# Segment maximum by block transposes, weights and dot sums by four chunks, and VectorE's window loop written out

## The reference

```python
x = _layernorm(x + _L0_gnn_ref(x, ...))    # sum of neighbours, two 256x256 weights
x = _layernorm(x + _L1_gnn_ref(x, ...))    # two GAT layers, 4 heads
x = _layernorm(x + _L2_gnn_ref(x, ...))    # three HGT layers, 8 heads, and a dense block each
x = _layernorm(x + _L3_gnn_ref(x, ...))    # typed and weighted sum of neighbours

# GAT, once per layer
e = leaky_relu(el[src] + er[dst]); ex = exp(e - segment_max(e, dst)[dst])
out = segment_sum(z[src] * ex / segment_sum(ex, dst)[dst], dst)
# HGT, once per layer
scores = sum(Q[dst] * kt, -1) / scale * mu;  e = exp(scores - segment_max(scores, dst)[dst])
agg = segment_sum(V[src] * e / segment_sum(e, dst)[dst], dst)
```

## Time and profile before

| what | value |
|---|---|
| median of 3 executions | 7095.4 us (7089.9 to 7103.44) |
| the profiled execution, its time | 7100.4 us |
| the profiled execution, its span | 7098.4 us |
| mean granted TensorE clock | 0.787 of full |
| busy share PE, DVE, ACT, POOL | 69%, 63%, 39%, 61% |
| GAT stages in the span | about 1530 to 2230 and 2230 to 3050 us, with the dense work ahead of the second |
| HGT stages in the span | windows from 3078.6, 4201.1 and 5328.5 us on, some 730 us each |

### The profile page before, as it was taken

The page is one execution under the profiler, slowest core; times in us unless marked ns, Lnnn a source line. Parts: engine busy times, 40 slices in busy tenths (PEclk is TensorE's granted clock), DMA queues, the critical chain, the costliest instruction groups (busy, mean ns, idle before and its releaser), DMA issues. The chain is left out here.

```text
span 7098.4 us, 101999 instructions
## 1 busy us (share of the span) xinstructions
PE 4898.9 (69%) x25668; PEld 3603.3 (51%) x25669; DVE 4452.5 (63%) x10705; ACT 2794.8 (39%) x6632; POOL 4296.3 (61%) x4216
## 2 busy tenths in 40 slices
PE   3780267657775777567767977776986676896665
PEld 2670144435554555455545965554874454673343
DVE  7550222256666666879996458898448999664334
ACT  1220000036665665455554655444665455450000
POOL 0777577747774777367774247775227777216775
PEclk6665565668887888789998988889998989896665
DMA  1220133343442335255554245555225555323334
GB/s 35 97 84 5 44 99 99 99 81 104 105 99 73 105 104 98 95 175 158 163 160 93 68 129 159 159 158 128 65 90 167 160 160 159 81 90 114 98 98 90
DMA packets 353408, 771.53 MB, mean 109 GB/s; under 512 B 88772, under 2 KB 199265, under 8 KB 349745
## 3 DMA queue, kind: packets, MB, share of 16 engines
q0 software_dynamic: 213760, 613.91, 33.0%
q1 hardware_dynamic: 139441, 155.22, 6.6%
HBM read 662.95 MB, written 105.92 MB: 108 GB/s over the span
## 5 line engine op out<-in xcount | busy, mean ns | idle before, releaser
L719 POOL DMA_INDIRECT ring<-tab_kv,idx_i x1392 | 1386.6, 996 | 638.3 <-issue 386.7
L1110 PE MATMUL pp<-ring,oh 128*128 128x256 f32 x1856 | 866.3, 619 | 434.4 <-DMA ring<-tab_h,idx_i 208.4
L719 POOL DMA_INDIRECT ring<-tab_z,src_i x928 | 919.4, 991 | 380.6 <-issue 254.7
L797 PE MATMUL pp<-ring,X 128*128 128x264 f32 x2784 | 898.9, 459 | 110.6 <-DVE ring L699 96.2
L1110 PEld LDWEIGHTS pp<-ring,oh 128*128 128x128 f32 x1856 | 506.9, 300 | 793.4 <-issue 391.6
L760 PE MATMUL pq<-Qs,oht 128*128 x7020 | 749.2, 244 | 181.5 <-issue 106.1
L849 ACT ACTIVATE ohb<-iota_row,lo_s 128x128 bf16<-128x128 f32 x2360 | 751.6, 390 | 41.6 <-PEq L731 23.4
L760 PEld LDWEIGHTS pq<-Qs,oht 128*128 128x128 bf16 x7020 | 554.0, 103 | 419.7 <-issue 285.9
L797 PE MATMUL pp<-ring,scratch 128*128 128x264 f32 x1856 | 673.2, 504 | 128.8 <-DVE ring L699 127.8
L699 DVE TENSOR_TENSOR ring<-ring 128x512 f32<-128x512 f32 x899 | 698.5, 783 | 55.0 <-ACT ring L888 54.9
L1018 DVE TENSOR_TENSOR acc<-acc,pp 128x264 f32 x1160 | 491.0, 423 | 352.1 <-PE pp L797 273.7
(11 more groups left out here) (306 smaller groups left out, 8338.9 us busy)
## 6 DMA issues: line engine op xcount, KB each, us to landing
...
ring<-tab_y,src_i POOLq DMA_INDIRECT x464, 2.8
ring<-tab_h,idx_i POOLq DMA_INDIRECT x464, 2.8
```

The costliest lines, as they stand in the source:

```text
L719: nc.gpsimd.indirect_dma_start(out=ring[:, par, c, :], out_offset=None, in_=table, in_offset=bass.IndirectOffsetOnAxis(ap=idx[:, w * WC + ...
L797: last = nc.tensor.matmul(pp[p % 2][:, 0:W8], oh[:, par % 2, 2 * p + c, :], ring[:, par % RW, 2 * p + c, 0:W8], start=(c == 0), stop=(c == 1))
L1110: last = nc.tensor.matmul(bank[:, 0:D], oh[:, b, 2 * k + c, :], ring[:, b, k, c, :], start=(c == 0), stop=(c == 1))
```

## The change

- The windows' small state on one partition (`conn`, `single`, `pL`, `pR`, `rF`, `rB`, `cL`, `cR`, `inL`, `inR`) is replaced. The penalties between chunks are laid out once, ahead of the layers, as a row of 68 values per window and spread over all 128 partitions by five matmuls with ones (`link`).
- The scores are kept head first, so that partition 16h + c is head h and chunk c. VectorE's transpose of 32x32 blocks then brings the last column of the forward scan, and the first of the backward one, into the rows of partitions 0, 32, 64 and 96, two heads in each. VectorE scans these on all partitions and transposes the results back into columns. TensorE's `T2` and `T3`, ScalarE's copy of the scores (L877) and the copy of the penalties (L953) go; VectorE reads the transposed scores from PSUM. `C.wait` stands between the dependent instructions.
- The rescaling factor comes by two matmuls more: `ratio` sums the masked differences into one row, `factor` builds 1 - oh + oh*exp, in PSUM, where `rescale` reads it without the copy of L998.
- A weight instruction and a dot sum take four chunks (128x1024 elements) in place of two. In HGT POOL does one of four quads in place of three of eight pairs.
- VectorE's windows are written out 29 times; TensorE's and ScalarE's stay in the loop.
- The orders by hand are new. `C1` to `C4` are now `T1`, `ratio`, `T4`, `factor`.

```diff
+        row_l = s.sb("row_l", [1, NW, 2, LH], BF16)
+                e.wait_ge(s_l, 1)
+                for k in range(parts):
+                    n = min(LW, NW - LW * k)
+                    nc.tensor.matmul(ptr[k][:, 0:n * 2 * LH], ones_r[:, :],
+                                     row_l[:, LW * k:LW * k + n, :, :].rearrange("o w h e -> o (w h e)"), start=True, stop=True
+                                     ).then_inc(s_b, 1)
+                    L.do(nc.vector.tensor_copy(link[:, LW * k:LW * k + n, :].rearrange("p w e -> p (w e)"), ptr[k][:, 0:n * 2 * LH]))
...
+    ORDER_V_DOTS = order("S0 S1 S2 W0 t S3 A0 W1 S4 A1 S5 A2 W2 S6 A3 S7 A4 D1 A5 D2 A6 D3 A7")
+    ORDER_V_SUMS = order("W0 t W1 A0 W2 A1 A2 L A3 W3 A4 D1 A5 D2 A6 D3 A7")
+    ORDER_T_DOTS = order("Q2 Q3 G0 T2 G1 Q4 Q5 T3 G2 Q6 Q7 G3 G4 C1 G5 N0 N1 G6 G7 C2 C3 H C4")
+    ORDER_T_SUMS = order("G0 Q2 Q3 G1 T2 G2 Q4 Q5 T3 G3 Q6 Q7 G4 C1 G5 N0 N1 G6 G7 C2 C3 H C4")
...
-            on_pool = (3, 5, 7) if dots else ()
+            on_pool = (3,) if dots else ()
+            def weigh_quad(eng, par, q):
+                v = ring[:, par % RW, 4 * q:4 * q + 4, 0:D].rearrange("p c (h x) -> p c h x", h=heads)
+                return eng.tensor_tensor(v, v, bc(ring[:, par % RW, 4 * q:4 * q + 4, D:D + heads], 3, D // heads), ALU.mult)
...
-                            if w >= 2 and q < len(on_pool):
-                                weigh(w - 2, par, q)
+                            if w >= 2 and q == 1 and on_pool:
+                                weigh(w - 2, par)
...
+                    def ratio(w, par):
+                        e.wait_ge(s_G, w + 1)
+                        nc.tensor.matmul(pc[1][0:1, 0:HD], one_c[:, :], G[:, :, :].rearrange("p k h -> p (k h)"),
+                                         start=True, stop=True).then_inc(s_Gm, 1)
+                    def T4(w, par):
+                        e.wait_ge(s_exp, w + 1)
+                        nc.tensor.transpose(sc_t, S1, ident[:, :]).then_inc(s_T4, 1)
+                    def factor(w, par):
+                        e.wait_ge(s_eg, w + 1)
+                        nc.tensor.matmul(fac, one_r[:, :], one_r[:, 0:HD], start=True, stop=False)
+                        nc.tensor.matmul(fac, oh[0:1, par % 2, 0, :], neg_r[:, 0:HD], start=False, stop=False)
+                        nc.tensor.matmul(fac, oh[0:1, par % 2, 0, :], gr[:, :], start=False, stop=True).then_inc(s_fac, 1)
...
+                    def red(w, par, q):
+                        e.wait_ge(s_mul, w * NPR + (2 * q + 4))
+                        k = 2 * (q % 2)
+                        nc.vector.tensor_reduce(scw[:, par % 2, :, 4 * q:4 * q + 4].rearrange("p h c -> p c h"),
+                                                prod[:, k:k + 2, :, :].rearrange("p k c (h x) -> p (k c) h x", h=HD),
+                                                AX.X, ALU.add).then_inc(s_red, 1)
...
-                        if p:
-                            red(w, par, p - 1)
+                        if p and p % 2 == 0:
+                            red(w, par, p // 2 - 1)
...
+                    def D1(w):
+                        C.base, C.n = c_base + w * c_per, 0
+                        e.wait_ge(s_T1, w + 1)
+                        C.do(nc.vector.tensor_tensor_scan(F, pens(w, 0), sc_t, -BIG, ALU.add, ALU.max))
+                        C.do(nc.vector.tensor_tensor_scan(R[:, ::-1], pens(w, 1)[:, ::-1], sc_t[:, ::-1], -BIG, ALU.add, ALU.max))
+                    def D2(w):
+                        C.wait()
+                        C.do(nc.vector.transpose(at_c(inF, 2), two(FR[:, P - 1:P + 31])))
+                        C.do(nc.vector.transpose(at_c(inR, 2), two(FR[:, P:P + 32])))
+                        C.wait(3)
+                        C.do(nc.vector.tensor_tensor_scan(flat(outF[:, :, :]), links(w), flat(inF[:, :, :]), -BIG, ALU.add, ALU.max))
+                        C.wait(4)
+                        C.do(nc.vector.tensor_tensor_scan(flat(outR[:, :, :])[:, ::-1], links(w)[:, ::-1],
+                                                          flat(inR[:, :, :])[:, ::-1], -BIG, ALU.add, ALU.max))
+                        C.wait(5)
+                        C.do(nc.vector.transpose(two(colF[:, :]), at_c(outF, 1)))
+                        C.wait(6)
+                        C.do(nc.vector.transpose(two(colR[:, :]), at_c(outR, 3)))
+                        C.do(nc.vector.tensor_copy(inF[:, :, 0], outF[:, :, 2 * WC]))
+                        C.wait(7)
+                        C.do(nc.vector.tensor_tensor_scan(F, pens(w, 0), sc_t, colF[:, 0:1], ALU.add, ALU.max))
+                        C.do(nc.vector.tensor_tensor(dg[:, :], outF[:, :, 1], outR[:, :, 2], ALU.subtract))
+                    def D3(w):
+                        C.wait(10)
+                        C.do(nc.vector.tensor_tensor_scan(R[:, ::-1], pens(w, 1)[:, ::-1], F[:, ::-1], colR[:, 0:1], ALU.add, ALU.max))
+                        C.wait(11)
+                        nc.vector.scalar_tensor_tensor(G[:, :, :], bc(dg[:, :], 1, HD // 2), 0.0, mine[:, :, :], ALU.min, ALU.mult
+                                                       ).then_inc(s_G, 1)
+                        C.wait(12)
+                        nc.vector.tensor_tensor(S1, sc_t, R, ALU.subtract).then_inc(s_sub, 1)
...
-                    windows(first, both, last_, e, RW)
+                    first(0, 0, 1)
+                    for w in range(1, NW):
+                        both(w, w % RW, w // RW + 1)
+                    last_(NW - 1, (NW - 1) % RW)
```

More of the change, by code:

```diff
@@ L589, in _ @@
                 L.do(nc.vector.memset(pen[:, :, :], 0.0))
-                L.do(nc.vector.memset(conn[:, :], -BIG))
+                L.do(nc.vector.memset(row_l[:, :, :, :], -BIG))
+                L.do(nc.vector.memset(ones_r[:, :], 1.0))
+                L.do(nc.vector.memset(one_r[:, :], 1.0))
+                L.do(nc.vector.memset(neg_r[:, :], -1.0))
+                L.do(nc.vector.memset(one_c[:, :], 1.0))
+                L.step(nc.vector.memset(mine[:, :, :], 0.0))
+                for k in range(HD // 2):
+                    L.do(nc.vector.memset(mine[32 * k:32 * k + 1, k, :], 1.0))
+                L.do(nc.vector.memset(conn[:, :], 1.0))
                 for f, o in enumerate((src_i, idx3_i, idx8_c, w_c, lo_s, dstc)):
@@ L608, in _ @@
                 L.wait()
-                L.do(nc.vector.tensor_scalar(conn[:, 1:CH], conn[:, 1:CH], -BIG, None, ALU.mult))
-                L.do(nc.vector.tensor_scalar(single[:, :], single[:, :], -BIG, None, ALU.mult))
+                for k in range(2):
+                    at = row_l[:, :, k, 1:LH - 1].rearrange("o w (c two) -> o w c two", two=2)
+                    for n, v in ((0, conn), (1, single)):
+                        L.do(nc.vector.tensor_scalar(at[:, :, :, n], v[:, :].rearrange("o (w c) -> o w c", c=WC), -BIG, None, ALU.mult))
+                L.wait()
+                e.sem_inc(s_l, 1)
+                for k in range(parts):
+                    n = min(LW, NW - LW * k)
+                    e.wait_ge(s_b, k + 1)
+                    L.do(nc.vector.tensor_copy(link[:, LW * k:LW * k + n, :].rearrange("p w e -> p (w e)"), ptr[k][:, 0:n * 2 * LH]))
                 L.wait()
@@ L658, in attend @@
         order_t = ORDER_T_DOTS if dots else ORDER_T_SUMS
-        width = D if dots else HD
         RW = 2
@@ L693, in attend @@
             NPR = WC // 2
-            on_pool = (3, 5, 7) if dots else ()
-            on_dve = [p for p in range(NPR) if p not in on_pool]
-            def weigh_pair(eng, par, p):
-                v = ring[:, par % RW, 2 * p:2 * p + 2, 0:D].rearrange("p c (h x) -> p c h x", h=heads)
-                return eng.tensor_tensor(v, v, bc(ring[:, par % RW, 2 * p:2 * p + 2, D:D + heads], 3, D // heads), ALU.mult)
+            on_pool = (3,) if dots else ()
+            on_dve = [q for q in range(NQ) if q not in on_pool]
+            def weigh_quad(eng, par, q):
+                v = ring[:, par % RW, 4 * q:4 * q + 4, 0:D].rearrange("p c (h x) -> p c h x", h=heads)
+                return eng.tensor_tensor(v, v, bc(ring[:, par % RW, 4 * q:4 * q + 4, D:D + heads], 3, D // heads), ALU.mult)
             exs = lambda par: ring[:, par % RW, :, D:W8]
@@ L724, in _ @@
                         gathers(w, w % RW)
-                    for w in (NW - 2, NW - 1):
-                        for k in range(len(on_pool)):
-                            weigh(w, w % RW, k)
+                    if on_pool:
+                        for w in (NW - 2, NW - 1):
+                            weigh(w, w % RW)
                 @blk.tensor
@@ L1035, in first @@
                             leaky(w, par, n)
-                        chain(w)
+                        D1(w)
+                        D2(w)
+                        D3(w)
                     def both(w, par, n):
```

197 lines of the change are left out of this document (67 added, 130 removed).

## The result

The changed kernel took 7116.4 us (median of 11 runs, 7103.5 to 7123.2) beside 7099.3 us for the kernel before (11 runs): ratio 1.0023, 95% interval 1.0014 to 1.0032. It is slower, as forecast, but by 17 us where the sum said 73.

What follows compares the result with a forecast made beforehand. GAT was taken as bound by POOL's issue of gathers, HGT by a ring of VectorE and TensorE. GAT +67, HGT 0 and setup +6 made +73 us: 7168 us (slower), own range 7120 to 7215, whole range 7000 to 7240.

Steps and rivals of the forecast that it cites:

- I take 0.48 x 4 = 1.9 us, since GAT's quads stand at many phases: GAT's gathers wait for VectorE's four long weight products, 0.48 us each on average; period +1.15 us, +67 us in all.
- 0.0 us: HGT's window: VectorE's savings and the new orders' idle time cancel; 87 x 0 = 0 us, bounds -183 and +190.
- chain, with the end of the stalls in it: VectorE's HGT scan chain: -1.4 us a window by shorter work, and 0.82 us of stalls under POOL's products gone.
- turn: idle ahead of S0 to S2: HGT, between windows: S0 and S2 wait for TensorE's matmuls and register reads; +2.5 us a window, bounds +1.3 and +3.3.
- G0 late: idle ahead of A0 and S4: HGT: TensorE's G0 waits for W0, now behind S2, so A0 and S4 wait; +1.2 us a window, bounds +0.3 and +2.0.
- idle ahead of A4 to A7: HGT, VectorE: half of the idle time ahead of the `A`s lies behind the chain's hand-overs and goes; -0.5 us a window.
- the chain's gain is taken back by the turn: HGT: the chain's -1.4 us a window is offset by the new orders' +2.5 us of idle time between windows.
- The setup: The penalties' stage ahead of the layers: five copies, five matmuls, a memset and four products more; +6 us.
- POOL's stop (23.4): HGT: POOL's gathers and waits for VectorE's quads would stop a gain at a period of 23.4 us, not reached.
- Quads cost no more than pairs: Rival: GAT's gathers lose nothing to the longer products and HGT stays; 7101 us, no change; chance 0.12.
- TensorE keeps up: Rival: TensorE's sequencer runs ahead of the scores' matmuls, HGT gains 1.6 us a window; 7029 us; chance 0.28.
- Upper bounds: Rival: the turn and G0's lateness cost their upper bounds, HGT 1.2 us a window longer; 7272 us; chance 0.15.

Runs made afterwards that it cites:

- octets: The changed kernel with GAT's weights in two instructions over eight chunks each in place of four over four; 7169.0 us, ratio 1.0113.
- b_quads_2: The kernel before with GAT's weights as four instructions over four chunks, in its own order; 7167.9 us, ratio 1.0118; first run, beside 7.99 to 8.01 ms, 1.002.
- b_unrolled_2: The kernel before with only VectorE's windows written out; 7087.9 us, ratio 0.9999; first run, beside 7.99 to 8.01 ms, 0.987.
- tiles_early: The changed kernel with TensorE's windows written out and the next window's eight tile numbers read ahead of the turn; 6955.0 us, ratio 0.9812.
- pairs_w0: The changed kernel with GAT's weights by pairs of chunks again and, in HGT, W0 ahead of S2; 6832.9 us, ratio 0.9643.
- h_first: The changed kernel with the scores' twelve matmuls ahead of two transposes in HGT; ratio 1.043 beside 7.99 to 8.01 ms; repeated, 7092.3 us, 1.0009.
- w0_first: The changed kernel with W0 ahead of S2 in VectorE's HGT order; ratio 0.998, beside a kernel before of 7.99 to 8.01 ms.

## Why the prediction was wrong

Right in the main by its mechanisms, wrong by its sum: +73 forecast, +22.8 in the spans. Two terms carry the miss, -26 us in GAT and -24 in HGT.

*GAT, "I take 0.48 x 4 = 1.9 us, since GAT's quads stand at many phases": the step that failed.* The mechanism is shown: gathers take 0.994 us on average with pairs, 1.042 with quads and 1.141 with octets. By the Trainium skill's sentence (SBUF — State Buffer, Who interferes with whom), that `tensor_tensor` was not found to stall such a DMA, neither the quads nor the octets would have cost anything; the runs decide against it for these gathers. The size was off: 16 gathers came out 1.53 us a window over their undisturbed time, not 1.9, and the period grew by some 0.8 us, not 1.15; the two stages by 40.7 us, not 67. The mean over all phases holds where phases do vary: W0 to W2 of the changed kernel cost 0.47 us each on average, 0.48 predicted. W3 follows an instruction that waits for a gather to land, and stands at phases that cost little, 0.11 us. (b_quads_2 gave 1.93 for its four, as the mean would have it, but two of them stand at nearly one phase each, so that is luck.) The order in the diff (`A2 L A3 W3`) would have told it.

*HGT, "0.0 us": a sum of terms, most of them near, some short.* For the 24 windows of the second HGT stage (time occupied is from an instruction's start to the next one's, less the idle time between), us a window:

| step | predicted | measured |
|---|---|---|
| dot sums | -0.24 | -0.26 (4.78 to 4.52) |
| weights, with the end of POOL's stalls | -0.53 | -0.54 (4.03 to 3.49) |
| chain, with the end of the stalls in it | -2.2 | -3.3 (6.17 to 2.91) |
| copy L998 and the rescaling | -0.2 | -0.46 |
| `S` and `A` themselves | 0 | +0.28 |
| turn: idle ahead of S0 to S2 | +2.5 | +2.3 |
| G0 late: idle ahead of A0 and S4 | +1.2 | +1.9 |
| idle ahead of A4 to A7 | -0.5 | 0.0 |
| idle within the chain, the rescaling, the rest | 0 | -0.5 |
| sum | 0.0 | -0.5 |

That the sum is within 0.5 us is in part luck. The chain, the idle time in it and the rescaling gained 1.8 us more than predicted and the turn 0.2, and G0's lateness, the idle time ahead of A4 to A7 (which stayed) and `S` and `A` took 1.5 back. Over all three stages HGT came out 0.3 us a window shorter.

The turn came out as worked out: 3.5 us idle ahead of S0 and S2 (3.4 predicted). The four matmuls of G0 take 2.12 us in the window shown, but in only 7 of the 24 windows over 1.9. The block transposes take 0.17 to 0.21 us (0.2 taken). The failed term is the chain: free of stalls, in GAT, it takes 2.9 us where I had 3.6, against 5.0 before (5.0). The durations were right, 3.8 us by the rows after against 3.95 (for fourteen instructions; the 15 of the prediction is a miscount), but they overlap by 0.9 us and not by 0.35. The first rows are of the old chain, the others of the new one:

```profile
4576.41 0.48 DVE L987 TENSOR_TENSOR_SCAN X<-penw,cc,X 128x128 f32<-128x128 bf16 x1
4576.93 0.48 DVE L988 TENSOR_TENSOR_SCAN X<-penw,cc,X 128x128 f32<-128x128 bf16 x1
```
```profile
4604.87 0.30 DVE L955 TENSOR_TENSOR_SCAN outF<-link,inF 128x68 f32<-128x68 bf16 x1
4605.08 0.27 DVE L957 TENSOR_TENSOR_SCAN outR<-link,inR 128x68 f32<-128x68 bf16 x1
4605.27 0.18 DVE L960 STREAM_TRANSPOSE colF<-outF 128x32 f32<-128x32 f32 x1
```

L988 needs the result of L987, directly ahead, and starts 0.04 us behind its end. L957 and L960 start 0.08 to 0.09 us before the end of the one ahead, and neither needs it: in the diff every `C.wait` but the first, ahead of which A5 stands, is for the last step but one or an earlier one, since forward and backward steps alternate. Of the eleven pairs of neighbouring steps ten overlap by 0.06 to 0.10 us, and the last, L972 and L975, by 0.02. No run changes the alternation alone, so its share is read from the rows. Also POOL's products had stalled more of the old chain than the one scan that I counted: 1.2 us, not 0.8, and the rescaling by 0.3. And G0's lateness costs 1.9 us and not 1.2, within its bounds.

*What I priced too low by far is what the order left unused.* I took the order as costing 2.5 + 1.2. That was nearly its cost, but as one mistake: W0 alone, one place earlier, gives 2.9 to 3.1 of it back. That a single move could do so I didn't see, since I priced the hole ahead of S2 and the wait for G0 as two things, where W0 is the filling of the one and the cause of the other. Beside the forecast's step "the chain's gain is taken back by the turn" this is shown: with W0 ahead of S2 the changed kernel's HGT is 3.4 us a window shorter than before, the chain and all other changes together.

*The setup:* from the first copy L601 to the first gather of `sum_edges` 14.4 us before, and 19.7 from the same copy after, so +5.3 us (+6 forecast); the 6.9 above hold the scatter of the stages between as well. The written-out loop was 0 in b_unrolled_2 (0 forecast). POOL's slack covered its own later gathers, as said; it ended at 23 us, where the prediction had put POOL's stop (23.4).

*The rivals.* "Quads cost no more than pairs" is refuted by 0.8 us a window. "TensorE keeps up" did not happen: S0 and S2 waited for it, but tiles_early and pairs_w0 show that 2 to 3 us a window lay exactly there. "Upper bounds" was near for G0 alone.

## What to carry to other kernels

A shorter chain is worth what stands behind its last step: here a gain of 3.3 us of VectorE's work was eaten by idle time, most of which one misplaced instruction made. Look in the order for work whose inputs are ready and which another engine needs soon, and put it into the hole. In a chain of short dependent steps let two independent halves alternate: a step that needs the one directly ahead started 0.04 us behind its end, the others up to 0.1 us before it. Merging instructions saves some overhead per piece, but where another engine waits for an instruction of VectorE to end, the wait grows faster than the length: the same work cost the gathers 0.75 us a window in eight pieces, 1.5 to 1.9 in four and 3.1 in two. A phase is not random when a wait ties the two engines together; follow what the instruction ahead waits for before taking a mean.

## What the runs showed beyond that

The first five kernels ran where the kernel before took 7.99 to 8.01 ms. Gathers and VectorE's instructions were as long as elsewhere (a gather 0.946 us, a pair's product 0.687), but engines woke late from waits, and TensorE's mean granted clock was lower: 0.75 for the kernel before and 0.73 for g_pairs, against 0.79 elsewhere. Timeline of g_pairs (the changed kernel with GAT's weights by pairs) in `sum_edges`, TensorE, then VectorE:

```profile
1534.46 2.07 PE L1101 MATMUL pp<-ring,oh 128*128 128x256 f32 x4 [1.53 <-DMA ring<-tab_y,src_i]
...
1544.51 0.42 DVE L1132 TENSOR_TENSOR acc<-acc,pp 128x256 f32 x1 [10.07 <-issue]
```

TensorE's sums end at 1536.53, and VectorE's addition of them starts 8 us later; POOL's gathers between them take 0.95 us as always. There g_pairs was at 1.032 (1.029 to 1.035), h_first at 1.043 (1.039 to 1.047), w0_first at 0.998 (0.996 to 1.001), b_unrolled at 0.987 (0.983 to 0.991) and b_quads at 1.002 (0.999 to 1.004). Of three that were repeated beside 7.09 ms none gave the same answer: 1.001 for h_first, 1.000 for b_unrolled, 1.012 for b_quads. Two expectations from there:

> The changed kernel, with each GAT weight instruction over four chunks issued as two over two chunks, back to back in the same place; HGT is as changed. If a gather waits for the end of the VectorE instruction with two SBUF operands that it meets, the part by which gathers come out longer falls from 1.52 us a window to about 0.75 and the GAT period from 21.55 to about 20.8 us: 58 x 0.75 = 44 us less than the changed kernel, some 7072 us, faster than before by 0.3 to 0.4%. If GAT became longer because of the new orders, the later first weight or the written-out loop, the period stays at 21.5 and the time at 7116.

> The changed kernel, with W0 ahead of S2 in VectorE's HGT order, as it was before. If G0's lateness is what A0 and S4 wait for (0.72 and 1.13 us idle), both waits go and W0 fills 1.1 of the 2.2 us ahead of S2: the period falls by up to 3 us, but not below POOL's 23.7, so by 1 to 2 us, 90 to 170 us in all, to 6950 to 7030 us. If TensorE's clock or POOL is behind these waits, S4's stays and the gain is under 50 us.

What did carry over is the length of the gathers in GAT, 1.000 us with pairs in g_pairs and 1.041 with quads in w0_first, and the worth of W0's place: g_pairs has the changed kernel's HGT and took 34.0 us a window, w0_first 31.1, so 2.9 us less, as beside 7.09 ms. Why the hand-overs were late there stays open; nothing in the kernels was changed to test it.
